# Attention beside an MLP on one core: stacks laid out in DRAM in their final form, values stored widened, nine equal attention steps, search products over 128 rows, x loaded into its rows

## The reference

```python
x = L0_attn_x
xn = _layernorm(x, axis=-1)
s = _L0_attn_ref(xn, w_qkv, w_out)          # 16 heads of 16, causal softmax, then @ w_out
g = _silu(_L0_ffn_ref(xn, W1, B1, W2, B2, LN_G, LN_B))
x = x + s * g
...
for i in range(6):                          # _L0_ffn_ref: 256 -> 1024 -> 256
    x = gelu(x @ W1[i].T + B1[i]) @ W2[i].T + B2[i] + x
    if i < 5: x = _layernorm(x, LN_G[i], LN_B[i])
```

## Time and profile before

| | us |
|---|---|
| median of 3 runs | 1853.83 (1852.13 to 1854.62) |
| the profiled execution | 1850.46 |
| its span, first to last instruction | 1848.7 |
| TensorE busy | 1700.0 (92%), mean granted clock 0.96 |
| VectorE busy | 1171.2 (63%) |
| ScalarE busy | 947.8 (51%) |
| GpSimd busy | 502.0 (27%) |
| DMA moved | 115.73 MB, 63 GB/s in the mean |

### The profile page before, as it was taken

The page is one execution under the profiler, slowest core; times in us unless marked ns, Lnnn a source line. Parts: engine busy times, 40 slices in busy tenths (PEclk is TensorE's granted clock), DMA queues, the critical chain, the costliest instruction groups (busy, mean ns, idle before and its releaser), DMA issues. The chain is left out here.

```text
span 1848.7 us, 29436 instructions
## 1 busy us (share of the span) xinstructions
PE 1700.0 (92%) x11216; PEld 1323.2 (72%) x11216; DVE 1171.2 (63%) x2644; ACT 947.8 (51%) x1380; POOL 502.0 (27%) x364
## 2 busy tenths in 40 slices
PE   6889999999989999999999999999999978789847
PEld 5678888788878888788888888788884333333336
DVE  5546777677867777677776777655544644446236
ACT  2344444455444454445544455444446866678823
POOL 1002333332333333233332332320112222222213
PEclk9889999999999999999999999999998988889979
DMA  5782020030030110300300203142004887787413
GB/s 196 259 215 42 12 41 13 21 41 13 12 53 9 29 31 12 49 13 12 47 7 21 47 7 46 22 63 36 1 9 71 139 133 116 123 132 123 96 56 136
DMA packets 91856, 115.73 MB, mean 63 GB/s; under 512 B 27208, under 2 KB 69832, under 8 KB 91656
## 3 DMA queue, kind: packets, MB, share of 16 engines
q1 hardware_dynamic: 91720, 113.90, 31.1%
HBM read 83.65 MB, written 30.15 MB: 62 GB/s over the span
## 5 line engine op out<-in xcount | busy, mean ns | idle before, releaser
L584 ACT ACTIVATE m_hid<-m_h_ps,m_b1s 128x512 f32<-128x512 f32 x384 | 264.5, 689 | 664.3 <-PE m_h_ps L673 619.0
L636 DVE TENSOR_TENSOR m_hidl<-m_hid,m_hidh 128x512 fp32r<-128x512 f32 x384 | 346.3, 902 | 351.2 <-ACT m_hidh L587 350.4
L840 ACT ACTIVATE a_prob<-a_st_ps 128x1024 f32<-128x1024 f32 x288 | 276.7, 1025 | 84.9 <-PE a_st_ps L878 82.5
L673 PE MATMUL m_h_ps<-m_xth,shared 128*128 128x512 f32 x768 | 285.9, 413 | 11.7 <-issue 9.3
L686 PE MATMUL m_y_ps<-shared,m_hidh 128*128 128x256 f32 x1536 | 284.5, 283 | 0.0
L587 ACT ACTIVATE m_hidh<-m_h_ps,m_b1s 128x512 fp32r<-128x512 f32 x384 | 260.7, 679 | 0.0
L686 PEld LDWEIGHTS m_y_ps<-shared,m_hidh 128*128 128x128 f32 x1536 | 248.7, 190 | 14.9
L546 POOL TENSOR_TENSOR xres<-xres,m_b2s 128x1024 f32<-128x1024 f32 x48 | 132.8, 2766 | 402.0 <-DVE xres L603 402.0
L686 PE MATMUL m_y_ps<-w2h,m_hidh 128*128 128x256 f32 x768 | 217.2, 283 | 0.0
L686 PE MATMUL m_y_ps<-shared,m_hidl 128*128 128x256 f32 x768 | 215.8, 281 | 0.0
L686 PE MATMUL m_y_ps<-w2l,m_hidh 128*128 128x256 f32 x768 | 214.6, 279 | 0.0
(11 more groups left out here) (111 smaller groups left out, 2944.1 us busy)
## 6 DMA issues: line engine op xcount, KB each, us to landing
mq<-q_parts SPq DMA_DIRECT2D x96, 128.0 KB, 4.8
mk<-k_parts SPq DMA_DIRECT2D x96, 128.0 KB, 7.5
shared<-q_parts SPq DMA_DIRECT2D x96, 128.0 KB
shared<-k_parts SPq DMA_DIRECT2D x96, 128.0 KB
q_parts<-mq SPq DMA_DIRECT2D x16, 512.0 KB, 5.8
k_parts<-mk SPq DMA_DIRECT2D x16, 512.0 KB, 3.2
raw<-w1t SPq DMA_DIRECT2D x48, 128.0 KB, 2.3
raw<-w2t SPq DMA_DIRECT2D x48, 128.0 KB, 2.2
```

The lines of the kernel that those rows point to most:

```text
L584: nc.scalar.activation(hid[n % 2][:], h_ps[n % 2][:], ACT.Gelu, bias=b1s[i % 2][:, k:k + 1])
L636: nc.vector.tensor_tensor(hidl[n % 4][:], hid[n % 2][:], hidh[n % 4][:].bitcast(F32), ALU.subtract).then_inc(low_done, 1)
L673: m = nc.tensor.matmul(h_ps[n % 2][:], w[i % 2][:, c, k * P:(k + 1) * P], x[t % 2][:, c, :], start=(c == 0 and w is w1h and x is xth), sto ...
L840: nc.scalar.activation(to, scores, ACT.Exp).then_inc(exp_done, 1)
```

## The change

- **x into its rows.** `project` loads all eight groups of x directly into `xres` at the start and normalises in place.
- **Values widened.** v is written with the ones beside it, as `values` [16 groups, 128, 8, 128], in four DMAs per group of tokens, 1.05 MB instead of 0.52. The attention loads 128 rows of 4 KB straight into `va`, issued before the stores at step 3; `augment` and `v_raw` are gone.
- **Stacks laid out in DRAM.** `lay_out_stacks` copies the parts of a group within DRAM to `q_stacks` and `k_stacks`, 128 rows as they shall lie in SBUF: twelve copies of 131 KB and two for the ones. Groups 0 and 1 are laid out at the start of `mlp`, group t+2 in slot t. The search and the attention then load a group in four DMAs, of 48 and of 50 rows of 8 KB. The shifts are stored into row 48 and 49 of each side in four DMAs of 8 KB.
- **Search over 128 rows.** In the MLP, q of side 1 is loaded into a buffer of its own (`x_apart`), and all rows that are not loaded hold zero (six fills by GpSimd at the start of `mlp`). A product over all 128 rows of q of one side and the full k gives the same scores. In the attention the visits still take 48 rows.
- **Nine steps.** The two narrow steps become one whose first exp is key tile 2 for both columns and whose second is key tile 6. Each step has two exps; the search visits are spread evenly.

```diff
-LOADS = 12
-NM_LOADS = 2
+LOADS = 4
...
+STORES = 2 * PARTS * 16
+def lay_out_stacks(sp, scratch, ones, n, laid):
     bt, hg = divmod(n, HG)
-    for to, src, order in ((to_q, scratch["q"], (0, 0, 1)), (to_k, scratch["k"], (0, 1, 0))):
+    for to, src, order in ((scratch["sq"], scratch["q"], (0, 0, 1)), (scratch["sk"], scratch["k"], (0, 1, 0))):
         for side in range(2):
             first = HG * HD * hg + PAIR * HD * side
             for r, part in enumerate(order):
                 rows = src[first:first + PAIR * HD, part, SEQ * bt:SEQ * (bt + 1)].rearrange("(c d) n -> d c n", d=HD)
-                to_rows = to[SIDE * side + r * HD:SIDE * side + (r + 1) * HD, :, :]
-                sp.dma_start(to_rows.bitcast(F32), rows).then_inc(loaded, 16)
+                sp.dma_start(to[n, SIDE * side + r * HD:SIDE * side + (r + 1) * HD, :, :], rows).then_inc(laid, 16)
...
+def load_stacks(sp, scratch, to_q, to_k, n, loaded):
+    for to, src in ((to_q, scratch["sq"]), (to_k, scratch["sk"])):
+        for side in range(2):
+            rows = slice(SIDE * side, SIDE * side + ROWS)
+            sp.dma_start(to[rows, :, :].bitcast(F32), src[n, rows, :, :]).then_inc(loaded, 16)
...
-    sp.dma_start(keep["v_raw"][n % 2][:], rows).then_inc(keep["v_loaded"][n % 2], 16)
-def augment(nc, pool, keep, n):
-    pool.wait_ge(keep["v_loaded"][n % 2], 16 * (n // 2 + 1))
-    nc.gpsimd.tensor_copy(keep["va"][n % 2][:, :, :, 0:HD], ...).then_inc(keep["v_ready"], 1)
+    sp.dma_start(keep["va"][n % 2][:], scratch["v"][n].rearrange("p t (h d) -> p t h d", h=HG)).then_inc(keep["v_loaded"][n % 2], 16)
...
-                rows = slice(SIDE * side, SIDE * side + STACK)
-                i = s.nc.tensor.matmul(s_ps[:, side, c * keys:(c + 1) * keys], s.q[m % 2][rows, first + c, qt * P:(qt + 1) * P],
+                rows = slice(0, P) if whole else slice(SIDE * side, SIDE * side + STACK)
+                i = s.nc.tensor.matmul(s_ps[:, side, c * keys:(c + 1) * keys], s.of_side(m, side)[rows, first + c, qt * P:(qt + 1) * P],
...
-                sp.dma_start(xin[g % 2][:], xg[g]).then_inc(x_loaded[g % 2], 16)
+                sp.dma_start(xres[:, TILES * g:TILES * (g + 1), :], xg[g]).then_inc(x_loaded[g], 16)
...
+            for g in range(2, GROUPS):
+                load_x(g)
             for g in range(GROUPS):
-                if g + 2 < GROUPS:
-                    sp.wait_ge(normed, g + 1)
-                    load_x(g + 2)
...
-                sp.dma_start(vd.rearrange("(g j p) d -> g p j d", p=P, j=TILES)[g], vout[g % 2][:]).then_inc(v_stored[g % 2], 16)
+                for hg in range(HG):
+                    values = vout[g % 2][:, :, HG * hg:HG * (hg + 1), :].rearrange("p j h d -> p j (h d)")
+                    sp.dma_start(vd[HG * bt + hg, :, first:first + TILES, :], values).then_inc(v_stored[g % 2], 16)
...
             load_bias(0)
+            for n in range(2):
+                lay_out_stacks(sp, scratch, keep["ones"], n, keep["laid"])
+            sp.wait_ge(keep["laid"], 2 * LAYING * 16)
+            sp.wait_ge(cleared, 6)
             for m in range(2):
                 search.load(sp, m)
...
+                if t + 2 < N_GROUPS:
+                    lay_out_stacks(sp, scratch, keep["ones"], t + 2, keep["laid"])
...
+    return [[part(0)], [part(1), part(3, BANK - P)], [far(0)], [part(2), part(6, BANK // 2)],
+            [far(1)], [far(2)], [far(3)], [part(4)], [part(5), part(7, BANK - P)]]
...
                     if n and n + 1 < N_GROUPS:
                         sp.wait_ge(st_done, NU * n)
+                        sp.wait_ge(search.stored, STORES * (n + 2))
                         load_stacks(sp, scratch, qs[(n + 1) % 2], ks[(n + 1) % 2], n + 1, keep["qk_loaded"][(n + 1) % 2])
-                        sp.wait_ge(search.stored, 16 * (n + 2))
-                        load_shift(sp, scratch, qs[(n + 1) % 2], n + 1, keep["qk_loaded"][(n + 1) % 2])
-                        sp.wait_ge(keep["v_ready"], n)
+                if step == 3 and n:
+                    sp.wait_ge(av_done, NS * n)
+                    if n + 1 < N_GROUPS:
                         load_values(sp, scratch, keep, n + 1)
-                if step == 2 and n:
                     store_o(n - 1)
```

More of the change, by code:

```diff
@@ L135, in __init__, with of_side @@
         s.at = {visit: i for i, visit in enumerate(s.visits)}
+    def of_side(s, m, side):
+        return s.apart[m % 2] if side and m < AHEAD else s.q[m % 2]
     def load(s, sp, m):
@@ L140, in load, with pe_visit @@
             sp.wait_ge(s.done, s.at[m - 2, NP - 1] + 1)
-        load_stacks(sp, s.scratch, s.q[m % 2], s.k[m % 2], m, s.loaded[m % 2])
+        for side in range(2):
+            rows = slice(SIDE * side, SIDE * side + STACK)
+            sp.dma_start(s.of_side(m, side)[rows, :, :].bitcast(F32), s.scratch["sq"][m, rows, :, :]).then_inc(s.loaded[m % 2], 16)
+            sp.dma_start(s.k[m % 2][rows, :, :].bitcast(F32), s.scratch["sk"][m, rows, :, :]).then_inc(s.loaded[m % 2], 16)
     def store(s, sp, m):
         sp.wait_ge(s.maxed, 2 * s.at[m, NP] + 2)
-        sp.dma_start(s.scratch["nm"][m].rearrange("a h (t q) -> (a h t) q", q=P), s.nmt[:]).then_inc(s.stored, 16)
-    def pe_visit(s, pe, s_ps, v):
+        for part in range(PARTS):
+            for side in range(2):
+                first = part * HG * QT + side * PAIR * QT
+                row = SIDE * side + STACK + part
+                to = s.scratch["sq"][m, row:row + 1, :, :].rearrange("a c (t q) -> a (c t) q", q=P)
+                sp.dma_start(to, s.nmt[first:first + PAIR * QT, :]).then_inc(s.stored, 16)
+    def pe_visit(s, pe, s_ps, v, whole):
         m, p = s.visits[v]
@@ L230, in project @@
         b = Bufs(nc, ctx)
-        xin = [b.sb(f"p_xin{u}", [P, TILES, DIM]) for u in range(2)]
         w_raw = b.sb("p_w_raw", [P, HALVES, 3 * DIM])
@@ L741, in attend @@
     AT = {}
-    weights = [0.5 if WIDTH[step] < BANK else 1.0 for step in range(NS)]
-    total = sum(weights) * (N_GROUPS - 2)
     for v in VISITS:
-        due = total * (v - VISITS[0]) / len(VISITS)
-        at = 0
-        while due >= weights[at % NS]:
-            due -= weights[at % NS]
-            at += 1
-        AT.setdefault(at, []).append(v)
-    STEP_OF = {v: at for at, visits in AT.items() for v in visits}
+        AT.setdefault(NS * (N_GROUPS - 2) * (v - VISITS[0]) // len(VISITS), []).append(v)
     with ExitStack() as ctx:
@@ L832, in _ @@
                 n, step = divmod(at, NS)
[L833 to L836 removed]
+                for u in range(2):
+                    act.wait_ge(st_done, NU * n + 2 * step + u + 1)
+                    if u == 0 and at >= BUFS:
                         act.wait_ge(av_done, at - BUFS + 1)
[L838 to L839 removed]
+                    by_side = prob[at % BUFS][:].rearrange("p (s c) n -> p s c n", s=2)
+                    if step == FOURS:
+                        to, scores = by_side[:, :, :, BANK // 2 * u:BANK // 2 * (u + 1)], st_ps[u][:].rearrange("p s (c n) -> p s c n", c=PAIR)
+                    else:
+                        to, scores = by_side[:, :, u, :], st_ps[u][:]
                     nc.scalar.activation(to, scores, ACT.Exp).then_inc(exp_done, 1)
@@ L884, in values @@
                 n, step = divmod(at, NS)
-                half, parts = STEPS[step]
                 if DIAGONALS[step]:
@@ L1095, in gated_block @@
             "mk": [b.sb(f"mk{u}", [P, PAIR * SEQ], F32R) for u in range(2)],
-            "v_raw": [b.sb(f"v_raw{u}", [P, QT, HG * HD]) for u in range(2)],
             "va": [b.sb(f"va{u}", [P, QT, HG, 2 * HD]) for u in range(2)],
@@ L1113, in gated_block @@
             project(nc, x, wqkv, w1t, w2t, scratch, keep)
+            search.apart = stack_views([b.sb(f"x_apart{u}", [P, PAIR * SEQ], F32R) for u in range(2)])
             mlp(nc, w1t, w2t, b1, b2, ln_g, ln_b, scratch, keep, search)
```

146 lines of the change are left out of this document (64 added, 82 removed).

## The result

The changed kernel takes **1808.54 us** (median of 4 runs, 1807.84 to 1812.35), the kernel before in the same session 1854.22 (1852.13 to 1855.02). The ratio is 0.976, 95% interval 0.9743 to 0.9776: faster, by 46 us, where 98 were forecast, and above the range of 1720 to 1802. The profiled execution has a span of 1806.1 us against 1848.7.

A forecast was written before the change was run, and what follows sets the result against it. TensorE was taken to bound the MLP; projections and attention lost time to waits on late DMA transfers. Terms -19 + 4 - 35 - 48 = -98 us took 1853.8 to 1756 us, range 1720 to 1802.

The forecast's parts named there:

- Projections, -19: Projections stage: loading x straight into its rows removes VectorE's five waits, 22.9 us, of which 19 us were counted.
- 3.41 MB at 326 to 370 GB/s: Projections: DMA traffic per group takes 9.2 to 10.5 us, giving a cycle of 9.65 to 10.5 us.
- DMA-bound: Rival for the projections: they become limited by DMA, whole time 1761 to 1770 us; chance 0.1.
- Start of the MLP, +4 with an upper bound of 11: MLP start: layout copies and search loads ahead of the weight piece delay VectorE, costing 0 to 11 us, taken as 4.
- loads issued at 20, their 3.15 MB through at [...] 26 to 37: MLP start: us after stage start when search loads are issued and through, at 149 to 326 GB/s; weights just behind.
- Search products, -35: MLP search visits: 128-row products avoid the row-grouping change, saving 3.6 us a group over ten groups.
- Attention, -48: Attention stage: falls from 385.6 to 338 us, ended by the one DMA engine that carries the 17-row stores.
- Four search loads of 1.57 MB over sixteen 15: Attention: the search loads, spread over sixteen engines, add 15 us to the busiest engine's sum of 315.
- Stacks 1.64 MB/10/26 GB/s = 6.3: Attention: 50-row stack loads run on ten engines, giving the store-carrying engine 6.3 us a group, 88 over fourteen groups.
- the stage at 314: Attention, rival that nothing queues on one engine: ScalarE and TensorE bound it at 314 us, whole time 1732; chance 0.12.
- a stack load at 8 us: Attention, slow end of its term: stack loads costing 8 us make the stage 362 us, a gain of only 24.
- stack loads slow: Rival for the attention: stack loads run slowly or on few engines, whole time 1914 or 2109 us; chance 0.08.

The follow-up runs named there:

- e8: Changed kernel with the widened values held by groups of heads and stored in one DMA with 2 KB pieces instead of four with 512 B: 1798.48 us.
- e2: Changed kernel with the MLP's search products taking 48 rows of each side again, loads and buffers unchanged: 1834.41 us.
- e3: Changed kernel with each attention group's four 17-row stores made as four of 16 rows and one of the four sum rows: 1747.92 us.
- e9: Changed kernel without the four pairs of search loads in the attention, so the search there multiplies older stacks: 1776.67 us.
- e12: Changed kernel with each 50-row stack load of the attention split into one of 48 rows and one of 2: 1808.69 us.
- e10: Changed kernel with 2 KB value pieces in one DMA, early weights and first search load, 16-row stores and 128-row stack loads in the attention: 1720.25 us.
- e4: Changed kernel with the attention's stacks loaded as two DMAs of 128 rows instead of four of 50, 28 percent more bytes: 1779.81 us.
- e7: Kernel before the change, with only its 17-row attention stores made as four of 16 rows and one of the sum rows: 1808.16 us.

## Why the prediction was right in part and wrong in its size

The sign was right, and each of the four terms moved the way that was forecast; each was sized too well, in sum by 54 us of 98. Three of them lie outside their own ends (-12.1 against -14, +15.5 against +11, -22.4 against -24). The step that failed is in each case the price of a transfer or of a visit, taken from a row of another shape or from a single one; the largest is the queue of the attention.

- **Projections, -19, measured -12.1.** The wait for x went, and the cycle is 9.25 us, as near the 370 GB/s bound as I could ask; VectorE alone gained 22.5 us. The step that failed is "3.41 MB at 326 to 370 GB/s": I took the rate of the stores of q and k, with pieces of 2 KB, for the widened values, with pieces of 512 B. The queue did not slow the cycle but stood behind it, and the stage ended 17.7 us after VectorE began the last low half of k, instead of 7.3, a tail for which the sum had no term. With larger pieces the term is -20.9 (e8). The rival "DMA-bound", 5 to 14 us above my figure, is what happened, with 7.
- **Start of the MLP, +4 with an upper bound of 11, measured +15.5** (the first two slots took 52.7 us instead of 37.2). The step that failed is "loads issued at 20, their 3.15 MB through at [...] 26 to 37": the 28 copies took 18.9 us to issue where I had 13 (my own row of 24 loads in 12.9 makes 0.54 each, not the 0.46 that I used), and the first load went out 21.9 after the stage's start, and the 3.15 MB ran at the slow bound, 150 GB/s, another 21 us and more. I took the value near the fast end because 48 rows are three times as many as 16; they ran no faster (150 against the 149 of the earlier trace rows). That choice is one error, and the bound above it was low as well, since copies and their landing had been put at 16.
- **Search products, -35, measured -25** (e2). The sign of it came: the first product behind a visit takes 0.23 us, and with 48 rows again the time comes back. The size rested on one visit of the earlier trace rows; the medians over all chunks between 200 and 1290 us, before and after, are 3.42 and 3.28 us with a visit of 512 columns, 3.35 and 3.16 for 384, 3.42 and 3.30 for four of 256, 3.34 and 3.20 for four of 128, which makes 3.0 a group and not 3.6. Of these 30 us, 3 go at the five layer boundaries, where one chunk takes 5.15 us in the mean instead of 4.49; what it waits for the profile does not show. Some 2 us I have not traced.
- **Attention, -48, measured -22.4.** The engine that carries the 17-row stores ends the stage, as forecast: without such stores it is 55.7 us shorter (e3). The step that failed is what else this engine was given. "Four search loads of 1.57 MB over sixteen 15": leaving them out saves 30 (e9). "Stacks 1.64 MB/10/26 GB/s = 6.3": the 26 GB/s an engine is what one engine does alone, ten of them at 50 rows do 201/10 = 20. At that rate a group's stacks take 8.2 us, 27 more in 14 groups. With the 15 of the search loads this is 42 where 25 are missing (363 - 338), so the two overlap, and how they share the 25 no run separates: the loaded engine works part of its queue alone, and there it may feel nothing of the slow rate. e12 shows that the way I weighed a load, by its bytes on each engine, is not the one that counts: this engine got a fifth less of the stacks, and nothing was gained.
- Without the engine I had the stage at 314; e3 has 307.5 and e10 298.7. The groups were forecast rightly: in e10 the exps run over 290 us, with 17.8 to 18.2 a group behind a first one of 20.8. What was too long is the end, for which I kept the 22.7 us of the earlier trace rows: they were the 17-row stores themselves, and without them it is 7.
- The bad end of the attention term, 362 with "a stack load at 8 us", came close to the 363.2 by luck in part: it left the search loads at 15. The rival "stack loads slow" (1914) was the right worry at the wrong size: 201 GB/s, where it decided below 123.

What I did not ask is whether the 17-row stores could go. The 10.7 us a group stood in my sum as a given, 171 of its 315 us.

## What to carry to other kernels

Work out for each repeated DMA how many engines it runs on, and look at the busiest engine's queue before touching anything else: a row count of 17 in a store cost 56 us here, and one more DMA that takes the odd row away gave as much on the old kernel as the whole change. A load that is spread over all 128 rows may carry a quarter more bytes than needed and still be through sooner; here it moved them at twice the rate. Place first in a queue what is needed first, and price a load by a row of its own shape, in rows and in size of pieces, or keep the slow bound.

## What the hardware showed that I had not expected

- More engines do not make a load of few rows faster: 201 GB/s on 50 rows with ten engines, 166 on 48 and 2 with sixteen, 403 on 128 with sixteen. Eight 48-row loads in a row (150 GB/s) are no faster than 24 of 16 rows (149 in the earlier trace rows).
- The largest divisor up to sixteen holds for 50 rows: a share of 0.64 while only such loads are under way. The Trainium skill (DMA: Bandwidth & Descriptors, Why a DMA increments its semaphore by 16 and not by 1) gives this rule for engines; no run contradicts it, but the time followed the rows.
- Work queued ahead can stop the engine that issues: for the same four stores of 17 rows SyncE needed 1.20 us in one group and 12.57 in the next, 1.37 at that place with the 128-row stack loads of e4, and 1.81 for four of 16 rows in e3. It is not the row count alone: four stores of 16 rows took 6.92 us in e7 behind 24 loads of 16 rows.
- Stores in pieces of 512 B instead of 2 KB cost 7.4 us in a stage of 106 with the same bytes: 299 GB/s against 383 in a window with every engine busy.
